# A two-layer decoder on one core: the layer norms' last scaling moved from VectorE to ScalarE

## The reference

```python
def _layernorm(x, axis=-1, eps=1e-05):
    m = jnp.mean(x, axis=axis, keepdims=True)
    v = jnp.var(x, axis=axis, keepdims=True)
    return (x - m) / jnp.sqrt(v + eps)

x = _layernorm(x + _L0_attn_ref(...))     # norm 1
x = _layernorm(x + _L0_xattn_ref(...))    # norm 2
x = _layernorm(x + _L0_ffn_ref(...))      # norm 3
x = _layernorm(x + _L1_attn_ref(...))     # norm 4
x = _layernorm(x + _L1_xattn_ref(...))    # norm 5
x = _layernorm(x + _L1_ffn_ref(...))      # norm 6, the output
```

## Time and profile before

| | us |
|---|---|
| median of 3 runs | 2263.66 |
| lowest, highest of them | 2257.88, 2267.17 |
| the profiled execution | 2256.6 |
| its span, first to last instruction | 2254.6 |
| PE, DVE, ACT, POOL busy | 1949.8, 1416.5, 817.8, 971.9 |

### The profile page before, as it was taken

One profiled execution on the slowest core, in us unless ns is written; L12 is line 12 of the kernel. 1 busy time (PEld: TensorE's weight loads), 2 busy tenths in 40 slices (PEclk: granted clock), 3 DMA queues, 4 the chain that ended last, 5 costly groups with the idle time before them and its releaser, 6 DMA issues.

```text
span 2254.6 us, 40952 instructions
## 1 busy us (share of the span) xinstructions
PE 1949.8 (86%) x14696; PEld 1498.9 (66%) x14696; DVE 1416.5 (63%) x3800; ACT 817.8 (36%) x1665; POOL 971.9 (43%) x988
## 2 busy tenths in 40 slices
PE   5686889898888889888898888989889898989997
PEld 3453568667766677566686676766767666767886
DVE  5555667656775577755766557764677656775554
ACT  2222333334333434324343343333433334433442
POOL 2202443455335553336434463344533555335554
PEclk7677899999999999899999999999999999999998
DMA  5000000000000000000000000000000000000000
GB/s 166 25 0 1 14 13 1 1 2 25 3 1 1 4 26 1 1 3 15 15 1 1 1 25 4 1 2 2 25 4 1 1 1 1 4 1 1 1 3 4
DMA packets 24110, 22.68 MB, mean 10 GB/s; under 512 B 16266, under 2 KB 22132, under 8 KB 23412
## 3 DMA queue, kind: packets, MB, share of 16 engines
q1 hardware_dynamic: 23892, 19.89, 3.2%
HBM read 18.83 MB, written 1.05 MB: 9 GB/s over the span
## 4 chain that ended last, share of the span: by engine, by line
PE 50%; DVE 22%; issue 17%; POOL 7%; ACT 3%; DVEq 0%; POOLq 0%; ACTq 0%
POOL xp_l L1336 4%; PE ps L901 4%; PE ps L916 4%; PE ps L917 3%; PE ps L918 3%; PE ps L903 3%; PE ps L902 3%; POOL pr_l L1336 3%; PE ps L872 3%; PE ps L1062 3%; DVE xmax_x L1685 3%; PE ps L1049 2%; PE ps L1050 2%; DVE smax L1603 2%; PE ps L867 1%
## 5 line engine op out<-in xcount | busy, mean ns | idle before, releaser
L1336 POOL TENSOR_TENSOR xp_l<-xp 128x512 f16<-128x512 f32 (+1 forms) x672 | 670.9, 999 | 1030.5 <-ACT xp L1220 1029.9
L1220 ACT ACTIVATE xp<-ps 128x512 f32<-128x512 f32 (+1 forms) x672 | 379.4, 565 | 711.0 <-PE ps L903 710.5
L1685 DVE TENSOR_REDUCE xmax_x<-ps 128x1 f32<-128x512 f32 x576 | 394.8, 688 | 277.4 <-PE ps L872 257.2
L1336 POOL TENSOR_TENSOR pr_l<-pr 128x512 f16<-128x512 f32 (+1 forms) x248 | 250.6, 1031 | 215.4 <-ACT pr L1176 197.3
L916 PE MATMUL ps<-xp,cx_tok 128*97 128x256 bf16 (+1 forms) x624 | 177.1, 284 | 7.8 <-ACT xo_x L1230 7.6
L916 PE MATMUL ps<-xp,c_tok 128*97 128x256 bf16 (+1 forms) x624 | 177.1, 284 | 7.4 <-ACT xo_x L1230 7.4
L917 PE MATMUL ps<-xp,c_tok 128*97 128x256 bf16 (+1 forms) x624 | 175.7, 282 | 0.0
L917 PE MATMUL ps<-xp,cx_tok 128*97 128x256 bf16 (+1 forms) x624 | 175.5, 281 | 0.0
L901 PE MATMUL ps<-xq_h,cx_hl 99*128 99x256 f16 (+1 forms) x624 | 175.5, 281 | 0.0
L901 PE MATMUL ps<-xq_h,c_hl 99*128 99x256 f16 (+1 forms) x624 | 175.4, 281 | 0.0
L903 PE MATMUL ps<-xq_h,cx_hl 96*128 96x256 f16 (+1 forms) x624 | 175.3, 281 | 0.0
(11 more groups left out here) (330 smaller groups left out, 4224.2 us busy)
## 6 DMA issues: line engine op xcount, KB each, us to landing
ct<-in_ctxT SPq DMA_DIRECT2D x8, 600.4 KB
raw_tok<-in_ctx SPq DMA_DIRECT2D x8, 576.0 KB
c_wg<-in_wg SPq DMA_DIRECT2D x1, 1088.0 KB, 7.8
c_wu<-in_wu SPq DMA_DIRECT2D x1, 1088.0 KB, 9.9
c_wd<-in_wd SPq DMA_DIRECT2D x1, 1088.0 KB, 5.0
xin<-in_x SPq DMA_DIRECT2D x8, 128.0 KB, 2.1
out<-ys SPq DMA_DIRECT2D x8, 128.0 KB, 1.9
c_wd<-in_sel SPq DMA_DIRECT2D x1, 768.0 KB
```

Source lines behind the costliest of these rows:

```text
L1220: fn(xp_slot(i, n)[0:k_, 0:w], bank(first_bank + n % 2, k_, 0, w), ACT.Exp, scale=scale).then_inc(xa_e[i].sem, 1)
L1336: sub = lambda out, a, b_: nc.gpsimd.tensor_tensor(out, a, b_, ALU.subtract)
L1685: red(cross.xmax[:, t, c:c + 1], bank(PART_BANK[q], P, 0, PARTS[c][1]), AX.X, ALU.max).then_inc(xa_xd[1].sem, 1)
```

## The change

DVE no longer scales. It makes a bias, minus the mean times the estimate, in one operation on 128 x 2 numbers, and raises a new semaphore `nw`. ACT waits for it in the norm's sixth piece and computes `Identity(scale * x + bias)` per tile, with the estimate and the bias as one number per partition. The shift of the bits and the subtraction become one operation (times -0.5, plus the constant). The wait for the previous store of `ys` moves from DVE to ACT. SP, POOL and PE have the same instructions as before, except that `xs_ready` now comes from ACT.

```diff
-STEPS = (114, 123, 328, 50, 41)
+STEPS = (110, 119, 316, 48, 39)
@@ ACT
+            def normalise(b, n, side, res):
+                for _ in range(NORM - 1):
+                    yield
+                if n == 6:
+                    act.wait_ge(x_out.sem, b.n * 16 + 16)
+                act.wait_ge(nw[n].sem, nw[n].at(b, 1))
+                y = side.nri[:].bitcast(F32)
+                for t in range(QT):
+                    m = fn(source[n][:, t, :], res[:, t, :], ACT.Identity, bias=side.nr[:, 1, t:t + 1], scale=y[:, t:t + 1])
+                m.then_inc(xs_ready[n].sem, 1)
+                yield
@@ ACT, experts (alike in the other parts)
-                for _ in range(NORM):
-                    yield
+                yield from normalise(b, 3, front, front.res[0])
@@ ACT, cross_steps
+                norm = None if b.known(0) else normalise(b.plus(-1), 5, cross, cross.res[b.plus(-1).odd])
...
                         exps(b, 1, h, p)
+                        if not b.known(0) and 5 <= NPAIR * h + p < 5 + NORM:
+                            next(norm)
@@ DVE, normalise
-                step(ts(nri[:], nr[:, 0, :].bitcast(I32), 1, None, ALU.logical_shift_right))
-                settle()
-                step(ts(nri[:], nri[:], -1.0, float(0x5F3759DF), ALU.mult, ALU.add))
+                step(ts(nri[:], nr[:, 0, :].bitcast(I32), -0.5, float(0x5F3759DF), ALU.mult, ALU.add))
...
-                if n == 6:
-                    dve.wait_ge(x_out.sem, b.n * 16 + 16)
-                for t in range(QT):
-                    m = ts(xs[:, t, :], res[:, t, :], mv[:, t, 0:1], y[:, t:t + 1], ALU.subtract, ALU.mult)
-                m.then_inc(xs_ready[n].sem, 1)
+                stt(q, mv[:, :, 0], -1.0, y, ALU.mult, ALU.mult).then_inc(nw[n].sem, 1)
```

More of the change, by code:

```diff
@@ L404, in decoder_kernel @@
         xs_ready = [count(f"xs_ready{n}") for n in range(7)]
+        nw = [count(f"nw{n}") for n in range(7)]
         def both(name, per):
@@ L1178, in self_attention @@
                         yield
-                for _ in range(1 + QUOTIENTS + NORM):
+                for _ in range(1 + QUOTIENTS):
                     yield
+                yield from normalise(b, 3 * i + 1, front, front.res[0])
             def context_high(b):
@@ L1249, in context_attention @@
                 yield
-                for _ in range(1 + NORM):
-                    yield
+                yield
+                yield from normalise(b, 2, front, front.res[0])
             def cross_start(b):
@@ L1288, in cross_end @@
                 yield
-                for _ in range(1 + NORM):
-                    yield
+                yield
+                yield from normalise(b, 5, cross, cross.res[b.odd])
             def experts(b):
@@ L1321, in last_ffn @@
                     yield
-                for _ in range(NORM):
-                    yield
+                yield from normalise(b, 6, front, front.res[0])
             def folding(_):
```

## The result

The changed kernel takes 2280.18 us (median of 10 runs, 2269.62 to 2285.0), the kernel before 2256.56 beside it (10 runs, 2242.4 to 2267.17). The ratio is 1.009, 95% interval 1.0073 to 1.0108: slower by 20 us (16 to 24). The forecast of 2278 us had 15.8 us of loss on a higher base: the three runs that it started from had a median of 2263.66. So the direction and the place were right, and the loss was larger than its sum. The profiled execution took 2283.9 us, its span 2281.8.

A forecast was written before the change was run, and what follows sets the result against it. PE was busy 86% of the span, the last-ending chain half PE and 22% DVE. Terms A to F summed to +15.8 us; with three runs counted against the profile, 2278 us, own range 2266 to 2290, 8 in 10: 2254 to 2295.

The forecast's parts named there:

- A: Norms 5 and 2: last feed-forward's copy waits behind norm 2's scaling; 2.5 us a batch, +15.0; also the stretch measured there.
- B: Norm 6, wait behind `ys`: DVE gains, exp held behind scaling; -0.7 us a batch, -4.2; also the stretch following A's.
- C: Norm 3: 1.41 us becomes 1.09 while PE's transposes wait; -0.3 us a batch, -1.8; also the stretch measured there.
- D: Norm 1: copy and casts behind the scaling move by 0.5 us a batch, +3.0; also the stretch measured there.
- at worst: In A: exps held for norm 5 delay POOL, norm 2's last Newton step meets a subtraction; bias 0.9 us later.
- the shift's 0.2 is lost again in the next meeting with POOL: Step in C, norm 3: the 0.2 us saved by dropping the shift operation brings no gain there.
- The sign that I named: Check for C: PE's wait ahead of norm 3's transposes should shrink by 0.3 us.
- E: Norm 4: next batch's copy comes behind the scaling, PE's product 0.55 us late in three batches; together +2.0 us.
- F: Norms without cover, four in batch 0 and the last two: +0.3 us each, +1.8 together.
- Faster: Rival: DVE's relief decides, copy at norm 2 loses under 1 us; 2255 or 2247 us; chance 0.16.
- No change: Rival: A's stalls are taken up, costing 0.5 instead of 2.5 us a batch; sum +3.8, 2267 us; chance 0.28.
- Slower still: Rival: held exps cost another 2 us in each of six batches; +28, 2292 us; chance within the forecast's 0.56.

The follow-up runs named there:

- e3: Kernel before, plus two extra copies on ACT (some 2.9 us) ahead of the last feed-forward's copy in batches 2 to 7; 2270.67 us, ratio 1.0092.
- e3a: Kernel before, plus one extra ACT copy of 1536 elements (1.46 us) ahead of the last feed-forward's copy; also called half-delay kernel; 2258.81 us, ratio 1.0004.
- e1: Changed kernel, but in batches 2 to 7 norm 2's scaling stands behind the last feed-forward's copy on ACT; 2252.8 us, ratio 0.9989.
- e5: Changed kernel with the first estimate back in its two old operations, so only the scaling moves to ACT; 2284.52 us, ratio 1.0118.
- e4: Changed kernel with the ACT scalings of norms 2, 4, 5 and 6 placed later; norms 1 and 3 stay; 2242.09 us, ratio 0.9947.
- e2: Kernel before with only the first estimate made in one operation; scalings stay on DVE; 2241.93 us, ratio 0.9948.
- e6: Changed kernel with norms 2, 4, 5 and 6 scaled later on ACT and norm 1's scaling back on DVE; 2239.53 us, ratio 0.9919.

## Why the prediction was right, and where it was not

The mechanism was right, but that 2278 lies so near the measured 2280.18 is luck: the base was some 6 us too high (2262.2 against 2256.56), and the loss added to it too small (15.8 against 20 to 24). Inside the sum, too, errors offset each other: A was far too small, and of the gain in B nothing is seen, while C gained more. For A to D together the forecast had 12.0 us, and the stretches have 23.8.

**A, norms 5 and 2.** The mechanism held and its size was too small. The stall grew by 4.05 - 0.56 = 3.49 us, at the top of the 2.6 to 3.5 that were given; the 0.55 counted as slack is 0.50 by e3 and e3a. That leaves 2.99, where I took 2.5: the "at worst" case, a Newton step that meets POOL, is what happens (0.96 at 838.21), in each of the six batches. The term that was missing is the clock: after the stall PE works 6.8 us at its lower level. A grew by 4.34 against e1 and A with B by 4.81; less 2.99, the clock costs about 1.3 to 1.8 a batch. With 1.2 measured for the first 3.4 us (e3a, e3) and 0.6 for the second (e5), that fits: 25.48, with 2.99 of stall, 1.8 of clock and the 0.27 that the estimate alone takes off A and B, makes 30.0, and the changed kernel has 29.83. Six times, A is 25 us longer than in the kernel before, and 26 (with B 29) longer than with the copy first, rather than 15.

**B, norm 6.** PE's wait behind `ys` fell as said (1.56 to 0.39 and 0.28), but the held exp and POOL's three subtractions in a row take most of it back: -0.25 without the stall ahead of it (e1), where the estimate alone has -0.19. I took -0.7, within 0 to -1.6. With the scaling later on ACT (e4) it is -1.0.

**C, norm 3.** The sum was -0.3 and it is -0.74. The step that failed is "the shift's 0.2 is lost again in the next meeting with POOL": the estimate alone brings -0.66. The rows say how: before, a Newton step met POOL's subtraction at 907.80, the maxima behind it came late, and PE waited for them. These rows of the kernel before show it:

```profile
907.80 1.04 POOL L1336 TENSOR_TENSOR xp_l<-xp 128x512 f16<-128x512 f32 x1 [0.51 <-ACT xp L1220]
...
907.93 0.93 DVE L1528 SCALAR_TENSOR_TENSOR nri_f<-nr_f,nri_f 128x2 f32<-128x2 f32 x1
...
909.73 0.39 PE L872 MATMUL ps<-c_hl,xq_h 99*128 99x512 f16 x1 [0.74 <-DVE xmax_x L1685]
```

In the changed kernel the counterpart of PE's product, at 930.97, has no wait. As I read it, the steps come 0.2 us earlier and miss that meeting. They are not rid of POOL: a step of the third round meets the next subtraction instead,

```profile
931.23 0.99 DVE L1542 SCALAR_TENSOR_TENSOR nri_f<-nr_f,nri_f 128x2 f32<-128x2 f32 x1
```

where its counterpart before took 0.16 (910.31). So the forecast's next meeting did come, but behind the maxima that PE waits for, and it took back only part of the gain. The move itself is worth -0.35 (e5), as forecast. The sign that I named, 0.3 less wait ahead of the transposes, was a bad one: it rose to 1.39, because PE got there earlier.

**D, norm 1.** +0.37 for +0.5, and the bias met POOL as said (0.54 at 1068.46). PE's wait for the copy behind the casts stayed at 2.07 and moved as a whole.

**E and F.** PE waits at most 0.19 for norm 4's copy, at four of the batch turns, less than the 0.55 given. Norms without cover cost +0.26 or +0.27 each, by PE's wait at five places, for +0.3. Batches 0 and 1 took 9.3 us longer in the changed kernel's profile than in that of before (to DVE's first work of batch 2: 460.5 against 451.2); but the half-delay kernel, which does there just what the kernel before does, took 459.8. What the change costs in those batches can't be told from one profiled execution each and stays open.

**The price of a scaling.** 0.47 us was forecast and 0.485 measured, though one of the two rows behind it was misread: L1296, with 64 elements, is a tanh and not an exponential.

**The rivals.** Faster: DVE's relief did not decide; the copy lost 3.5 us, not under 1. No change: of a stall only 0.5 us is taken up. Slower still was nearest in size beside the forecast: held exps cost (some 1.3 us a batch, by e4 against e1), and so does the clock, which neither it nor the forecast had.

## What to carry to other kernels

An engine works in its written order, so moving an operation to an idle engine puts its wait ahead of everything behind it there: find the next instruction in that queue that does not need it, see in the timeline how much earlier that one runs today, and put the moved operation behind it. With the same shorter estimate, the scalings in one order on ScalarE make the kernel 0.9% slower than before, and in another, with one norm left on VectorE, 0.8% faster. The estimate alone gives 0.5%, so these runs don't show that the move gains anything by itself, only what a bad place for it costs. And beside a stall of TensorE look at the granted clock behind it: here the first half microsecond added to the stall was free, and the lower clock cost 1.2 to 1.8 us on top of the rest.

## What the runs showed of the hardware

What PE's clock does behind a stall goes with the stall's length, but not with that alone: within one kernel, equal stalls went both ways. Behind the wait for this copy the clock went to the lower level in 0 of 30 batches with 0.56 us of wait (before, e1, e2, e4, e6), in 3 of 6 with 1.52, in 5 of 6 with 2.89 and in all 12 with 4.05 (changed, e5). A stretch of 3.4 us at the lower clock cost 1.2 us (e3a, e3), one of 6.8 us 0.6 more (e5). What else decides stays open.

Removing 0.2 us from a chain of small DVE operations gained 0.66 us at a place where, by the rows, it let them miss a subtraction of POOL ahead of PE's maxima; elsewhere on that chain it gained 0.2 (batch 0) or next to nothing (A).
